# New order of the attention work, second bias and gates moved into the expert loop

## The reference, cut to what matters

```python
xn = _layernorm(x)
# attention: 16 heads of 8
Qf, Kf = elu(xn @ Wq) + 1, elu(xn @ Wk) + 1
Kv, K1 = sum_l Kf[l] (x) V[l], sum_l Kf[l]            # per batch (8) and head
att = (Qf @ Kv) / (Qf . K1 + EPS) @ Wo
# experts: 8, of which each token uses its two best
probs = softmax(xn @ gate_w.T + gate_b)
topk_vals, topk_idx = top_k(probs, 2)
h = relu(xn @ w1[e] + b1[e])                           # 128 -> 256
expert_out[e] = h @ w2[e] + b2[e]                      # 256 -> 128
ffn = sum over the two chosen e of topk_vals * expert_out[e]
out = x + att + ffn
```

## Time and profile before

| | us |
|---|---|
| three runs: lowest, median, highest | 118.44, 119.11, 119.73 |
| the profiled execution, its own time | 117.28 |
| its span, first to last instruction | 115.5 |
| PE busy (share of the span) | 97.6 (85%) |
| DVE busy | 56.0 (49%) |
| ACT busy | 61.7 (53%) |
| POOL busy | 51.4 (44%) |

### The profile page before, as it was taken

One profiled execution on the slowest core, in us unless ns is written; L12 is line 12 of the kernel. 1 busy time (PEld: TensorE's weight loads), 2 busy tenths in 40 slices (PEclk: granted clock), 3 DMA queues, 4 the chain that ended last, 5 costly groups with the idle time before them and its releaser, 6 DMA issues.

```text
span 115.5 us, 2916 instructions
## 1 busy us (share of the span) xinstructions
PE 97.6 (85%) x780; PEld 90.2 (78%) x780; DVE 56.0 (49%) x222; ACT 61.7 (53%) x175; POOL 51.4 (44%) x62
## 2 busy tenths in 40 slices
PE   6948689991875799998999999999999999999600
PEld 6836578570574799987999999999999999999500
DVE  0789579699468475423253333443334433333400
ACT  4359768975031022223857586667766666676300
POOL 5016500477777769010000504123504557887870
PEclk9999999999999999999999999999999999999996
DMA  3995000001213821697446656757586787994522
GB/s 106 283 320 235 3 0 6 0 27 52 73 49 108 250 69 49 164 300 279 114 127 174 134 142 180 149 153 161 162 180 143 168 169 158 184 177 76 45 23 23
DMA packets 16703, 15.06 MB, mean 130 GB/s; under 512 B 1936, under 2 KB 16272, under 8 KB 16560
## 3 DMA queue, kind: packets, MB, share of 16 engines
q1 hardware_dynamic: 13584, 12.50, 36.6%
q0 software_dynamic: 2816, 2.18, 13.7%
q10 hardware_dynamic: 288, 0.20, 0.6%
HBM read 11.64 MB, written 3.23 MB: 129 GB/s over the span
## 4 chain that ended last, share of the span: by engine, by line
issue 28%; PE 23%; POOL 20%; DVE 13%; DMA 6%; ACT 4%; POOLq 2%; SPq 1%
POOL out L474 20%; DMA x_tok<-in_x 4%; PE banks L1037 4%; PE banks L1032 4%; PE banks L1007 4%; PE banks L917 3%; DVE kf L759 2%; PE banks L983 2%; DMA out<-res 2%; ACT xrow L511 2%; POOLq L115 2%; DVE qf L765 2%; PE banks L1018 2%; PE banks L945 1%; ACT xT L517 1%
## 5 line engine op out<-in xcount | busy, mean ns | idle before, releaser
L559 ACT ACTIVATE h<-banks,w_now 128x128 f32<-128x128 f32 x118 | 36.8, 364 | 17.3 <-PE banks L1068 17.3
L474 POOL DMA_INDIRECT out<-acc,token x16 | 25.0, 1562 | 34.5 <-DVE acc L807 33.0
L807 DVE SCALAR_TENSOR_TENSOR acc<-banks,xs,acc 128x128 f32 x59 | 20.7, 351 | 34.8 <-PE banks L1081 33.8
L1068 PE MATMUL banks<-xsT,w_now 128*128 x236 | 36.3, 277 | 0.4 <-issue 0.4
L1081 PE MATMUL banks<-w_all,h 128*128 x236 | 36.0, 276 | 0.0
L1068 PEld LDWEIGHTS banks<-xsT,w_now 128*128 128x128 f32 x236 | 30.9, 192 | 0.9 <-issue 0.8
L1081 PEld LDWEIGHTS banks<-w_all,h 128*128 128x128 f32 x236 | 30.9, 192 | 0.4 <-issue 0.2
L459 POOL DMA_INDIRECT sorted_dram<-xrow,slot x16 | 16.7, 1046 | 5.8 <-issue 4.6
L543 ACT COPY attT<-banks 128x512 f32<-128x512 f32 x4 | 2.3, 585 | 11.7 <-PE banks L1018 11.7
L917 PE MATMUL banks<-wkvg_f,xT 128*128 128x136 f32 x32 | 5.2, 294 | 3.2 <-ACT xT L517 2.6
L917 PEld LDWEIGHTS banks<-wkvg_f,xT 128*128 128x128 f32 x32 | 4.1, 189 | 4.2 <-ACT xT L517 3.0
(11 more groups left out here) (100 smaller groups left out, 111.6 us busy)
## 6 DMA issues: line engine op xcount, KB each, us to landing
w_now<-in_w1b SPq DMA_DIRECT2D x59, 129.0 KB, 2.3
w_all<-in_w SPq DMA_DIRECT2D x1, 1032.0 KB, 5.7
out<-res SPq DMA_DIRECT2D x4, 256.0 KB, 4.2
xs<-sorted_dram SPq DMA_DIRECT2D x3, 276.0 KB, 4.0
x_tok<-in_x SPq DMA_DIRECT2D x3, 256.0 KB, 4.8
xs<-sorted_dram SPq DMA_DIRECT2D x2, 138.0 KB, 2.5
x_tok<-in_x SPq DMA_DIRECT2D x2, 128.0 KB, 2.4
sorted_dram<-xrow,slot POOLq DMA_INDIRECT x16, 2.6
```

Of the source, the lines that this page charges most:

```text
L474: nc.gpsimd.indirect_dma_start(out=out_rows, out_offset=bass.IndirectOffsetOnAxis(ap=token[:, s:s + 1], axis=0), in_=acc[:, s * D:(s + 1) ...
L559: nc.scalar.activation(h[:, i % NH, c, :], h_ps[i % NHP][:, c * P:(c + 1) * P], ACT.Relu, bias=w1_now[:, i % NW, H + c:H + c + 1]).then_in ...
L807: nc.vector.scalar_tensor_tensor(out=mine, in0=y_ps[i % NYP], scalar=xs[:, bass.ds(goff, 1)], in1=mine, op0=ALU.mult, op1=ALU.add).then_in ...
L1068: last = nc.tensor.matmul(h_ps[i % NHP][:, c * P:(c + 1) * P], w1_now[:, i % NW, c * P:(c + 1) * P], xsT[:, bass.ds(toff, P)], start=True, ...
```

## The change

- The second bias is no longer a product. `w2` in SBUF has 128 more columns per expert that hold `b2` (row of 384 instead of 258 values; one load of 1.5 times the size), and a new DVE instruction per visit, `take_y`, adds it to the second product and writes `y` to SBUF (two buffers). `accumulate` then reads `y` instead of PSUM. On DVE `take_y(i+1)` stands before `accumulate(i)`.
- The gate of a visit is no longer read from the row by an address. POOL copies the gates out of the sorted rows (`take_gates`), PE transposes them and multiplies by the one-hot matrix `is_visit` (`transpose_gates`, `pick_gates`), DVE copies both results. This is done twice: for the first 4 sorted tiles and visits 0 to 7, then for all 16 and the other visits. The table loses its third row, and a row its last padding value.
- The late gate transposes, their copy by ACT, the eight bias instructions in each `project_out` and the three late filler products go. No filler products stand between the last `project_out` and the rows.
- New order on ACT, DVE and PE, with other PSUM banks and other waits: the ranks follow each other on PE, the four attention blocks run closer together, and the table is made after them (DVE: after `finish_q(3)` and beside `divide(2)` and `divide(3)`). `give_back` waits for tokens and base stores once, ahead of tile 0.

```diff
+    GATE_TILES, GATE_VISITS, GATE_GROUPS = [4, T], [(0, 8), (8, NI)], [2, len(XGROUPS)]
...
-            sp.dma_start(b2_f[:], b2_blocks).then_inc(b2_in, 16)
...
+            def take_gates(half):
+                first, end = (0, GATE_TILES[0]) if half == 0 else GATE_TILES
+                if half:
+                    pool.wait_ge(gatesT_done, 1)
+                nc.gpsimd.tensor_copy(gates[:, first:end, :],
+                                      xs[:].rearrange("p (s c) -> p s c", c=ROW)[:, first:end, D + 1:D + 1 + E]
+                                      ).then_inc(gates_done, 1)
...
             for n in range(len(XGROUPS)):
                 token_numbers(n)
+                if n + 1 in GATE_GROUPS:
+                    take_gates(GATE_GROUPS.index(n + 1))
...
+            def keep_gates(half):
+                rows = GATE_TILES[half] * E
+                dve.wait_ge(gatesT_done, half + 1)
+                nc.vector.tensor_copy(gatesT[0:rows, half, :], gatesT_ps[0:rows, :]).then_inc(gatesT_copied, 1)
+
+            def keep_picked_gates(half):
+                a, b = GATE_VISITS[half]
+                dve.wait_ge(gate_of_done, half + 1)
+                nc.vector.tensor_copy(gate_of[:, a:b], gate_of_ps[:, a:b]).then_inc(gate_of_copied, 1)
+
+            def take_y(i, woff):
                 dve.wait_ge(l2_done, i + 1)
+                if i >= 2:
+                    dve.wait_ge(acc_done, i - 1)
+                nc.vector.tensor_tensor(y[:, i % 2, :], y_ps[i % NYP], w2_all[:, bass.ds(woff + KC * D, D)], ALU.add
+                                        ).then_inc(y_done, 1)
+
+            def accumulate(i, toff):
+                dve.wait_ge(y_done, i + 1)
+                dve.wait_ge(gate_of_copied, 1 if i < GATE_VISITS[0][1] else 2)
                 mine = acc[:, bass.ds(toff, D)]
                 if i:
                     dve.wait_ge(acc_done, i)
-                nc.vector.scalar_tensor_tensor(out=mine, in0=y_ps[i % NYP], scalar=xs[:, bass.ds(goff, 1)], in1=mine,
+                nc.vector.scalar_tensor_tensor(out=mine, in0=y[:, i % 2, :], scalar=gate_of[:, i:i + 1], in1=mine,
                                                op0=ALU.mult, op1=ALU.add).then_inc(acc_done, 1)
...
             shares()
-            choose(0)
-            late_shift()
             pair_starts()
             places(1, slice(0, 4))
+            late_shift()
             finish_k(0)
             finish_k(1)
-            places(2, slice(4, T))
             mask_kv(0)
             finish_q(0)
+            places(2, slice(4, T))
+            mask_kv(1)
+            finish_k(2)
+            divide(0)
+            finish_q(1)
             choose(1)
             late_gates()
...
+            mask_kv(2)
             finish_k(3)
...
+            divide(1)
             finish_q(2)
             mask_kv(3)
             finish_q(3)
-            divide(1)
+            visits()
             divide(2)
+            order_visits()
+            divide(3)
+            keep_table()
             residual(0)
-            divide(3)
             residual(1)
             residual(2)
...
+            copy_xsT(1)
+            keep_gates(0)
+            keep_picked_gates(0)
+            take_y(0, woffs[0][0])
             for i in range(NI):
-                if i == 0:
-                    copy_xsT(1)
+                if i == 3:
+                    copy_xsT(3)
                 if i == 4:
-                    copy_xsT(3)
...
+                    keep_gates(1)
+                if i == 5:
+                    keep_picked_gates(1)
+                if i + 1 < NI:
+                    take_y(i + 1, woffs[(i + 1) // LOADS][(i + 1) % LOADS])
+                accumulate(i, toffs[i // LOADS][i % LOADS])
...
+            def transpose_gates(half):
+
+                pe.wait_ge(gates_done, half + 1)
+                tiles = GATE_TILES[half]
+                pe.wait_ge(xsT_dve, half + 1)
...
+            def pick_gates(half):
+
+                pe.wait_ge(gatesT_copied, half + 1)
...
-                for j in range(4):
-                    nc.tensor.matmul(wo_ps[k][:, j * P:(j + 1) * P], gatesT[:, k * P:(k + 1) * P],
-                                     b2_f[:, j * P:(j + 1) * P], start=(j == 0), stop=False)
...
-                    pe.wait_ge(acc_done, i - NYP + 1)
+                    pe.wait_ge(y_done, i - NYP + 1)
...
             rank_rows(0)
+            rank_rows(1)
+            rank_rows(2)
             project_k(1)
-            rank_rows(1)
             project_q(0)
-            rank_rows(2)
+            keys_values(0)
+            keys_values(1)
             project_k(2)
+            numerator(0)
             project_q(1)
-            keys_values(0)
+            keys_values(2)
             project_k(3)
+            numerator(1)
+            transpose_att(0)
             project_q(2)
+            keys_values(3)
+            project_q(3)
+            numerator(2)
+            numerator(3)
+            transpose_att(1)
             order_visits()
...
+            project_out(0)
             make_table()
...
-            warm_up(3, where=late_warm_ps)
...
+            transpose_att(2)
             project_out(1)
+            transpose_att(3)
+            project_out(2)
+            pe.wait_ge(table_done, 1)
             toffs = offsets_of(mybir.EngineType.PE, 1, 0, T_TOP)
...
                     first_product(i, toffs[i % LOADS])
+                if i == 0:
+                    transpose_gates(0)
                 if i == 1:
                     transpose_rows(2)
+                if i == 2:
+                    pick_gates(0)
+                if i == 6:
+                    transpose_gates(1)
+                if i == 7:
+                    pick_gates(1)
```

More of the change, by code:

```diff
@@ L43, in pair_key, with shape_constants @@
     return (i + BIAS_OF_KEY) * (j + BIAS_OF_KEY)
[L46 removed]
+def shape_constants(D, E, T, wrow):
     rows = np.arange(D)
@@ L434, in gate_values @@
                                         ALU.add).then_inc(row_done, 1)
-                nc.gpsimd.tensor_tensor(gates[:, EARLY, :], gated[:, EARLY, 0, :], gated[:, EARLY, 1, :],
-                                        ALU.add).then_inc(gates_done, 1)
             def fill_rows():
@@ L582, in _ @@
             exp_k(0)
-            for b in range(4, 6):
+            for b in range(4, B):
                 copy_v(b)
             exp_k(1)
-            copy_v(6)
-            copy_v(7)
             exp_q(0)
@@ L592, in _ @@
             exp_k(3)
+            copy_attT(0)
             exp_q(2)
             exp_q(3)
-            copy_gatesT()
-            for k in range(NBLK):
+            for k in range(1, NBLK):
                 copy_attT(k)
@@ L751, in late_gates @@
                                         ).then_inc(row_dve_done, 1)
-                nc.vector.tensor_tensor(gates[:, LATE, :], gated[:, LATE, 0, :], gated[:, LATE, 1, :], ALU.add
-                                        ).then_inc(gates_dve_done, 1)
             def finish_k(k):
@@ L880, in _ @@
                     toffs[j // LOADS] = offsets_of(mybir.EngineType.DVE, 1, j, T_TOP)
-                if j % LOADS == 1 and j < NI:
-                    goffs[j // LOADS] = offsets_of(mybir.EngineType.DVE, 2, j - 1, G_TOP)
+                if j % LOADS == 1 and j - 1 < NI:
+                    woffs[(j - 1) // LOADS] = offsets_of(mybir.EngineType.DVE, 0, j - 1, W_TOP)
         @block.tensor
@@ L985, in keys_values @@
                 last.then_inc(kv_done, 1)
-            def transpose_gates():
-                pe.wait_ge(table_done, 1)
-                pe.wait_ge(gates_done, 1)
-                pe.wait_ge(gates_dve_done, 1)
-                for k in range(NBLK):
-                    last = nc.tensor.transpose(gatesT_ps[:, k * P:(k + 1) * P],
-                                               gates[:, blk_tiles(k), :].rearrange("p t e -> p (t e)"), ident_t[:])
-                last.then_inc(gatesT_done, 1)
+            def transpose_gates(half):
+                pe.wait_ge(gates_done, half + 1)
+                tiles = GATE_TILES[half]
+                pe.wait_ge(xsT_dve, half + 1)
+                nc.tensor.transpose(gatesT_ps[0:tiles * E, :], gates[:, 0:tiles, :].rearrange("p t e -> p (t e)"),
+                                    ident_t[:]).then_inc(gatesT_done, 1)
+            def pick_gates(half):
+                pe.wait_ge(gatesT_copied, half + 1)
+                a, b = GATE_VISITS[half]
+                rows = GATE_TILES[half] * E
+                nc.tensor.matmul(gate_of_ps[:, a:b], gatesT[0:rows, half, :], is_visit[0:rows, a:b],
+                                 start=True, stop=True).then_inc(gate_of_done, 1)
             def numerator(k):
@@ L1162 @@
     T = x.shape[0] * x.shape[1] // P
-    row = D + 1 + E + 1
+    row = D + 1 + E
     w1 = np.asarray(L0_ffn_w1).transpose(1, 0, 2)
@@ L1171 @@
     w1b[:, :, H:H + H // P] = b1
-    b2_blocks = np.zeros((4, E, 4, D), dtype=np.float32)
-    for t in range(4):
-        b2_blocks[t, :, t] = np.asarray(L0_ffn_b2)
```

133 lines of the change are left out of this document (54 added, 79 removed).

## The result

The changed kernel took 120.73 us (median of 20 runs, 119.56 to 123.32), the kernel before 118.66 (20 runs, 117.41 to 121.06): the ratio is 1.018 [1.014, 1.022]. It is slower. Ratios compare the fast runs of each kernel alone, so they are not the quotients of the medians. The forecast was 118.7, a gain of 0.4 us; instead some 2 us were lost. 120.73 lies in the range, towards the slow end, but only because the range took in the rival of the clock.

A forecast was written before the change was run, and what follows sets the result against it. Attention work on PE, not the rows, was taken to set the start of the expert loop. The terms -4.35 + 2.6 + 1.35 gave -0.4 us, so 119.11 became 118.7 us, own range 117.6 to 119.7, with rivals 117.2 to 121.3.

The forecast's parts named there:

- the rival of the clock: PE's pause before the rows lowers its clock, slowing the first loop products: +1.0 us, 119.7 us; chance 0.32.
- step 4: Gate work inside the expert loop: four small PE operations and their waits for DVE copies, +2.6 us (1.5 to 3.2).
- Step 1: Attention on PE: 5.0 us of bias products and fillers gone, PE ends near 43.3, covered by the wait for rows.
- Step 2: Dispatches on POOL: ranks go first on PE, so dispatch 0 comes 1.2 us earlier and the last starts near 42.1.
- Step 3: Table later (40.3), w1 loads meet the last dispatches; rows only 0.25 us earlier, first product at 49.0: -4.35 us.
- the rival of undelayed dispatches: Last dispatches land undelayed, so rows come 1.2 us earlier, not 0.25: 117.7 us, or 117.3; chance 0.18.
- Step 5: DVE in the loop: take_y and accumulation take 0.86 us a visit against PE's 0.89, just covered, cost 0.
- the rival of VectorE: VectorE becomes the bound of each loop visit: +3.3 us, 122.0 us; chance 0.14.
- Step 6: End of the kernel: accumulations behind the next visit's take_y and late offset loads delay the last give_back, +1.35 us (0.9 to 1.7).

The follow-up runs named there:

- e1_fill: Changed kernel plus 18 filler products on PE between the last output product and the row transposes: 119.25 us, ratio 1.003 to the kernel before.
- e0_after: The changed kernel unchanged, run again as base line beside other runs on one chip: 120.17 us, ratio 1.014 to the kernel before.
- e6_pick_later: Changed kernel with 18 fillers and later late-gate work, plus pick_gates(1) at i == 11 instead of 10: 116.66 us, ratio 0.990 to the kernel before.
- e2_late_gates: Changed kernel with the late gate work two to three visits later on PE and DVE, no fillers: 118.43 us, ratio 0.987 to the kernel before.
- e10_no_fill: e7_pick_tail without the filler products ahead of the rows: 117.87 us, ratio 1.002 to the kernel before.
- e5_rows_first: Changed kernel with fillers and later gate work, plus row groups 0 to 2 loaded ahead of first weights 3 to 5: 118.58 us, ratio 1.003.
- e8_rows_stores: e7_pick_tail with the load order of e5_rows_first, and base stores behind visit 7's weights: 116.92 us, ratio 0.989 to the kernel before.
- e4_tail: Changed kernel with fillers and later gate work, plus the last seven accumulations ahead of the next take_y: 117.33 us, ratio 0.995.
- e4b_loads: Changed kernel with fillers and later gate work, plus VectorE's last two offset loads at visits 49 and 50, not 53 and 54: 117.57 us, ratio 0.998.
- e7_pick_tail: e6_pick_later and e4_tail together, with the fillers: 116.60 us, ratio 0.991 to the kernel before.

## Why the prediction was wrong

**What failed: step 4.** "Sum 2.6" for the gate work should have been 4.8, the excess of e1_fill's visits 0 to 7 over the kernel before with the clock up: 1.15 at visit 0, where I had about 0.45, and 10.34 - 6.69 = 3.65 behind it (3.71 in e0_after), where I had about 2.15. The waits were named rightly and sized rightly: PE stood 0.23 us (e1_fill, at 50.06), 1.39 for the row copy and 0.54 for the gates' copy, 2.16 where 0.2, 1.15 and 0.75 make 2.1 (the last two add up to 1.2 and 0.8 by their own terms). What failed is the rest. The four operations, put at 0.5, came to 1.0: from the start of each to the product behind it 0.22 and 0.32 in e1_fill's visit 0, 0.23 (58.43 to 58.66) and 0.27 (60.35 to 60.62) in e0_after. And some 1.6 us had no term at all. In e0_after the three second products of visits 4 to 6 end 2.78, 1.93 and 1.67 us after the one ahead of them, where 0.89 is a visit: 3.71 over. The two waits are 1.93 of it and the two operations 0.50. Some 0.75 is lost because products no longer overlap at the stops: in the running loop a group of four starts 0.45 us after the one ahead, though it takes 0.61, and the first one behind a stop takes 0.71. The last 0.53 is the stop for "issue" at 61.82. It stands right behind PE's offset load of 0.60 us, which began at 60.7 and ended when the products ahead of it ran out, at 61.30. e6_pick_later, where `pick_gates(1)` stands away from the load, has neither this stop nor the wait beside it.

In the kernel before PE made the same 16 loads, and the one wait for "issue" that the profile gives its products from 53 to 110 us is the 0.39 ahead of the first. The Trainium skill ("Advanced Engine Details and Errata", Sequencer Loop) says that engine instructions can be read and queued while the sequencer does other work. The kernel before agrees, with no such wait in its running loop; e0_after shows 0.53 us where a stop had left only four products ahead of the load.

**What failed second: the weights of the cases.** The clock fell, which was the rival at 0.32, under the forecast at 0.36. I argued that the pause lay at the length of 4.5 us after which the clock was seen low. It was 3.73, and the clock was at 0.50 by 46.00, 2.77 us after the last product. Without fillers it fell sooner in other executions: in e2_late_gates it was at 0.50 from 44.5, 1.25 us after the last product at 43.25, in e10_no_fill from 45.4, 1.54 us after 43.86. So the time since the last product, by which I judged, does not by itself tell when the clock falls. Its price, "+1.0" with bounds 0.3 and 2.8, was right in size: 0.92 and 1.27 us by the medians of two pairs, though 1.59 us in visit 0 of the traces (5.22 and 3.63). The Trainium skill's rule ("TensorE: Matmul & The Clock Gate", HAM oscillation) gave this case, and the traces of the four runs without fillers agree (0.50 at the first products).

With 4.8 for step 4 and the clock's 1.0 the forecast's own sum is -4.35 + 4.8 + 1.35 + 1.0 = +2.8; the traces give +2.64. That they meet so closely is partly luck: in these traces the front gained 0.76 more than forecast, and the clock cost 0.59 more. By the medians it is 2.07, as the first trace of the kernel before, at 117.28, is 1.4 us under its median of 20 and that of the changed kernel 0.8.

**What held.** Step 1: PE ended its attention at 43.23 (43.3 forecast) and waited for rows; the time is luck, as the table came 0.7 us earlier than forecast, and PE then stood 0.70 us ahead of `project_out(3)` (42.10), behind two offset loads of 0.78 and 0.83 us from 40.3 that had no term. Step 2: dispatch 0 came 1.25 us earlier (1.2); the last at 41.30, earlier than 42.1, as the 16 took 19.6 us. Step 3: the table at 39.59 (40.3, bounds 39.1 to 41.6), weights from 40.54 (41.2), the last dispatches 3.1 to 3.5 us to land (3.4), row loads at 44.79 (45.5), so the rival of undelayed dispatches fell. That the weights beside them are the reason fits the 2.4 to 2.6 us without any, but with half of them 2.74 (e5_rows_first) and 3.42 us (e8_rows_stores) were seen, so it is not shown. The first product at 48.25 is 0.75 earlier than forecast, which hid as much of the miss in this execution. Step 5: `take_y` 0.29 (0.28), and where VectorE alone sets the pace visits follow at 0.80 us (110.60 and 111.40), under PE's 0.89: the rival of VectorE fell. Step 6: 1.33 (1.35), but the sum was luckier than its shares: the order of the two instructions was put at 0.89 + 0.28 us, and e4_tail, which undoes it for the last seven visits, removed 0.59 (3.27 to 2.68). The rest was not taken apart; e4b_loads shows the row of `give_back`s passing a delay ahead of it on to the end.

**Open.** Four of the 20 runs of the changed kernel had a mean clock of 0.97 where most had 0.95, and took 119.7 to 122.3 us, so within one kernel the clock does not sort the times; where it fell in those runs no trace shows. Nor does one show what lowers it to 0.955 in many runs of the kernel before.

## What to carry to other kernels

When work moves into a loop in which the engine never stands, a wait costs more than its idle time: add the operation, the restart and every register load that the running loop had hidden, and put such work where the copy it needs was made visits ago. Work taken from the engine ahead of a wait leaves that engine idle; fillers in the pause were worth about 1 us here. With both mended, and the order at the end, the change does beat the kernel before, by 0.9% [0.4, 1.4] in e7_pick_tail; what PE then still waits for in the first visits is a weight load (0.56 us there, 1.25 in e8_rows_stores).

## What I had not expected of the hardware

The clock fell 1.2 to 2.8 us after the last product ahead of the rows, where a pause of 3 us had left it up; what tells the two apart is open. First weights of 129 KB took 2.1 to 5.7 us to land when issued beside rows and stores (e7_pick_tail), against a median of 2.7 us in mid loop in the same kernel. A pair of VectorE instructions, the second behind the first, goes through in 0.80 us, and in 0.68 us in the order of e4_tail, where I had put 0.86:

```profile
108.34 0.35 DVE L830 SCALAR_TENSOR_TENSOR acc<-y,gate_of,acc 128x128 f32 x1
...
109.02 0.35 DVE L830 SCALAR_TENSOR_TENSOR acc<-y,gate_of,acc 128x128 f32 x1
```
